# A graph layer on one core: the rows of a chosen block are selected in three pieces over three steps, and the program's end gets a new order

## The reference

```
edge_index = stack([src, dst]);  x_j = x[src];  x_i = x[dst]
msg = concatenate([x_i, x_j - x_i], axis=-1)
h = relu(msg @ W1 + b1)          # 64 -> 64
h = relu(h @ W2 + b2)            # 64 -> 128
h = relu(h @ W3 + b3)            # 128 -> 64
m = h @ W4 + b4                  # 64 -> 32
s   = segment_sum(m, dst, N)
cnt = segment_sum(ones, dst, N)
x = layernorm(x + s / maximum(cnt, 1))
```

## Time and profile before

| | us |
|---|---|
| median of 3 executions | 2438.02 (2434.82 to 2444.65) |
| the profiled execution | 2446.31 |
| its span, first to last instruction | 2444.5 |
| mean granted TensorE clock | 0.79 of full |
| TensorE matmuls busy | 1712.6 (70%) |
| GpSimd busy | 1128.2 (46%) |
| VectorE busy | 952.4 (39%) |
| ScalarE busy | 621.9 (25%) |

### The profile page before, as it was taken

One profiled execution on the slowest core, in us unless ns is written; L12 is line 12 of the kernel. 1 busy time (PEld: TensorE's weight loads), 2 busy tenths in 40 slices (PEclk: granted clock), 3 DMA queues, 4 the chain that ended last, 5 costly groups with the idle time before them and its releaser, 6 DMA issues.

```text
span 2444.5 us, 39204 instructions
## 1 busy us (share of the span) xinstructions
PE 1712.6 (70%) x13107; PEld 1103.7 (45%) x13107; DVE 952.4 (39%) x3083; ACT 621.9 (25%) x945; POOL 1128.2 (46%) x1168
## 2 busy tenths in 40 slices
PE   2242777777786777777677867777777777777796
PEld 2111544554454545454444554454544454544463
DVE  3673333333333333343333333333333333333354
ACT  2233222222222222222222222222222222222243
POOL 5276354445545453545455444545454544454412
PEclk7565887888878877888788888788888878788897
DMA  5343533443433434343434443443443343434341
GB/s 127 98 116 91 174 99 109 132 138 98 122 114 102 139 105 126 98 142 100 139 98 122 117 141 99 119 117 97 145 124 113 95 142 100 137 99 127 115 126 29
DMA packets 189929, 283.06 MB, mean 116 GB/s; under 512 B 84614, under 2 KB 90169, under 8 KB 189156
## 3 DMA queue, kind: packets, MB, share of 16 engines
q1 hardware_dynamic: 152341, 241.67, 31.9%
q0 software_dynamic: 36704, 37.00, 7.7%
q10 hardware_dynamic: 682, 1.85, 0.3%
HBM read 266.51 MB, written 13.73 MB: 115 GB/s over the span
## 4 chain that ended last, share of the span: by engine, by line
PE 40%; another core or an unknown queue 29%; issue 15%; DVE 8%; ACT 4%; DVEq 2%; DMA 1%; SPq 1%; POOL 0%; ACTq 0%; POOLq 0%
PE ps L954 21%; PE ps L978 4%; PE ps L986 4%; PE ps L994 2%; PE ps L1009 2%; DVE region L1384 2%; ACT work L713 2%; PE ps L898 2%; PE ps L968 2%; DVEq L1397 1%; PE ps L1006 1%; PE ps L916 1%; ACT work L721 1%; DVE region L1351 1%
## 5 line engine op out<-in xcount | busy, mean ns | idle before, releaser
L584 POOL DMA_INDIRECT xj<-z_rows,src_t x1107 | 1072.6, 969 | 1186.2 <-PE ps L916 682.0
L954 PE MATMUL ps<-region,x_p 128*96 128x150 bf16 (+53 forms) x5876 | 537.2, 256 | 244.9 <-issue 234.0
L954 PEld LDWEIGHTS ps<-region,x_p 128*96 128x96 bf16 x5876 | 479.2, 159 | 345.1 <-issue 337.3
L1351 DVE TENSOR_SCALAR region<-region,cst 128x1565 bf16<-128x1565 int16 (+6 forms) x416 | 242.3, 636 | 285.0 <-PE ps L954 151.2
L1366 DVE COPY work<-ps 128x512 f32<-128x512 f32 x194 | 133.4, 688 | 541.3 <-remote 380.7
L986 PE MATMUL ps<-work,w3s 128*64 128x512 f32 x784 | 327.0, 748 | 17.8 <-ACT work L721 14.5
L721 ACT ACTIVATE work<-ps,b2s 128x512 f32<-128x512 f32 x392 | 260.5, 686 | 249.4 <-remote 217.1
L994 PE MATMUL ps<-cst,work 128*128 128x128 f32 x784 | 150.5, 323 | 243.8 <-ACT work L728 224.1
L728 ACT ACTIVATE work<-ps,b3s 128x512 f32<-128x512 f32 x196 | 134.7, 687 | 720.1 <-remote 647.0
L978 PE MATMUL ps<-work,w2s 64*128 64x512 f32 x784 | 243.5, 700 | 39.2 <-ACT work L713 38.3
L713 ACT ACTIVATE work<-ps,b1s 128x512 f32<-128x512 f32 x196 | 134.7, 687 | 385.1 <-PE ps L898 312.2
(11 more groups left out here) (153 smaller groups left out, 907.6 us busy)
## 6 DMA issues: line engine op xcount, KB each, us to landing
dstb<-dst_rows SPq DMA_DIRECT2D x196, 252.0 KB
region<-src_rows SPq DMA_DIRECT2D x104, 391.2 KB
region<-src_rows SPq DMA_DIRECT2D x52, 407.2 KB
region<-src_rows SPq DMA_DIRECT2D x52, 403.2 KB
region<-src_rows SPq DMA_DIRECT2D x52, 376.2 KB
region<-src_rows SPq DMA_DIRECT2D x52, 375.8 KB
region<-src_rows SPq DMA_DIRECT2D x52, 374.0 KB
region<-src_rows SPq DMA_DIRECT2D x52, 366.2 KB
```

The source lines that it names most:

```text
L584: pool.indirect_dma_start(out=xj[:, u, j % UT, j // UT, 0:w], out_offset=None, in_=rows, in_offset=bass.IndirectOffsetOnAxis(ap=cols[:, j: ...
L954: chosen = nc.tensor.matmul(ps[0:XP, XBANK[h], lo - h * UE:hi - h * UE], xb[:, a, :], hot[:, q % QN, at + lo:at + hi], start=not begun[h], ...
L1351: nc.vector.tensor_scalar(hot[:, q % QN, 0:CW[c]], spread[:, q % QE, 0:CW[c]], cst[:, C_PID:C_PID + 1], None, ALU.is_equal).then_inc(s_hot, 1)
```

## The change

The selection of a chosen block's rows is cut into three pieces of chunks, `PIECES = [(0, 1, 2), (3, 4, 5), (6, 7)]`. TensorE does piece 0 in the step two before the block's own, piece 1 in the step before, both behind `sum_window` and ahead of layer 3, and piece 2 where the whole selection stood. VectorE builds the one-hots of a piece at the end of the step before, and SyncE loads the windows of the following block piece by piece, ahead of its other loads.

At the program's end: the engines meet only if another pass follows; each chunk's four matmuls of `messages` read four runs of neighbouring nodes, and `turn_messages` writes them back to their places; the short chunk comes last instead of first; every second chunk's addition of x goes from GpSimd to VectorE; and TensorE does matmuls whose result nobody reads (`stay_busy`) in the last steps and before the messages. A new assertion holds the chosen blocks at least three steps apart.

```diff
+PIECES = [(0, 1, 2), (3, 4, 5), (6, 7)]
-CHUNKS = [(0, NC % CH)] + [(NC % CH + CH * n, CH) for n in range(NC // CH)]
+CHUNKS = [(CH * n, CH) for n in range(NC // CH)] + [(NC - NC % CH, NC % CH)]
...
 (SyncE)
             def step(s):
-                if is_sorted(s) and STEPS[s] + 1 < SB:
-                    for c in range(CN - QN):
-                        load_windows(STEPS[s] + 1, QN + c)
+                for lead in range(3):
+                    if s + lead < S_N and is_sorted(s + lead) and STEPS[s + lead] + 1 < SB:
+                        for c in PIECES[2 - lead]:
+                            load_windows(STEPS[s + lead] + 1, c)
...
-                if s + 1 < S_N and is_sorted(s + 1) and STEPS[s + 1] + 1 < SB:
-                    for c in range(QN):
-                        load_windows(STEPS[s + 1] + 1, c)
...
-                sp.wait_ge(s_acc, added_by(S_N - 1))
-                sp.wait_ge(s_arrive, 4)
-                sp.sem_clear(per_pass)
-                sp.sem_inc(s_open, WIN)
                 with sp.If(off + WIN < end):
+                    sp.wait_ge(s_acc, added_by(S_N - 1))
+                    sp.wait_ge(s_arrive, 4)
+                    sp.sem_clear(per_pass)
+                    sp.sem_inc(s_open, WIN)
...
+            sp.wait_ge(s_acc, added_by(S_N - 1))
             sp.dma_start(cnt, sums[H3:H3 + 1, 0:N].rearrange("a (p c) -> a p c", c=NC)).then_inc(s_count, 16)
...
 (GpSimd)
             for n in range(len(CHUNKS)):
-                add_x(n)
+                if n % 2 == 0:
+                    add_x(n)
...
 (TensorE)
-            def selected_x(s):
+            def selected_x(s, piece):
...
-                free_x(s)
-                if b == 0:
+                if piece == 0:
+                    if copies_by(s - 1):
+                        pe.wait_ge(s_xc[0], copies_by(s - 1))
+                    if b:
+                        pe.wait_ge(s_xc[1], b)
+                    begun[0] = begun[1] = False
...
-                for c in range(CN):
+                for c in PIECES[piece]:
...
+            def stay_busy(n):
+                for k in range(n):
+                    nc.tensor.matmul(ps[0:XP, 0, :], xb[:, 0, :], x_p[:, 0:512], start=True, stop=True)
             def step(s):
                 if s < S_N:
                     if is_sorted(s):
-                        selected_x(s)
+                        selected_x(s, 2)
...
+                stay_busy({S_N + 1: 3}.get(s, 0))
                 if 2 <= s <= S_N + 1:
                     turn_layer3(s - 2)
+                stay_busy({S_N: 4, S_N + 1: 2, S_N + 2: 8}.get(s, 0))
                 if s >= 3:
                     sum_window(s - 3)
+                for lead in (1, 2):
+                    if s >= AHEAD and s + lead < S_N and is_sorted(s + lead):
+                        selected_x(s + lead, 2 - lead)
...
+            stay_busy(7)
+            pe.wait_ge(s_acc, added_by(S_N - 1))
             messages(0)
...
 (VectorE)
-                if s < S_N and is_sorted(s):
-                    for c in range(QN, CN):
-                        build_hot(STEPS[s], c)
...
-                for lead, some in ((2, (0, 1)), (1, (2, 3, 4))):
-                    if s + lead < S_N and is_sorted(s + lead):
-                        for c in some:
+                for lead in (1, 2, 3):
+                    if s >= AHEAD and s + lead < S_N and is_sorted(s + lead):
+                        for c in PIECES[3 - lead]:
                             build_hot(STEPS[s + lead], c)
...
+                    if n % 2:
+                        dve.wait_ge(s_m, n + 1)
+                        nc.vector.tensor_tensor(zc[:, cs, :], zc[:, cs, :], xc[:, cs, :], ALU.add).then_inc(s_z[1], 1)
```

More of the change, by code:

```diff
@@ L54 @@
     STEPS.append(k if n in SORTED_AT else SB + n - k)
+assert all(b - a >= 3 for a, b in zip(SORTED_AT, SORTED_AT[1:])) and FIRST_SORTED >= AHEAD + 3
 assert sorted(STEPS) == list(range(S_N)) and STEPS[-1] == S_N - 1
@@ L278, in build @@
         s_fin, s_m, s_z, s_sq, s_var, s_std, s_rstd, s_y, s_out = (
-            sem("messages"), sem("mean_message"), sem("z_ready"), sem("z_squared"), sem("var_ready"), sem("std_ready"),
+            sem("messages"), sem("mean_message"), [sem("z_ready_gpsimd"), sem("z_ready_vector")], sem("z_squared"), sem("var_ready"), sem("std_ready"),
             sem("rstd_ready"), sem("y_ready"), sem("out_stored"))
@@ L599, in _ @@
                 pool.dma_reset(range(s_gath[0].num, s_gath[-1].num + 1))
-                end_of_pass(pool, off)
-                pool.sem_inc(s_begun, 1)
                 with pool.If(off + WIN < end):
+                    end_of_pass(pool, off)
+                    pool.sem_inc(s_begun, 1)
                     for g in range(early):
@@ L609, in add_x @@
                 pool.wait_ge(s_m, n + 1)
-                nc.gpsimd.tensor_tensor(zc[:, at, :], zc[:, at, :], xc[:, at, :], ALU.add).then_inc(s_z, 1)
+                nc.gpsimd.tensor_tensor(zc[:, at, :], zc[:, at, :], xc[:, at, :], ALU.add).then_inc(s_z[0], 1)
             def normalise(n):
@@ L777, in _ @@
                     step(s)
-                end_of_pass(act, off)
-                act.sem_inc(s_begun, 1)
                 with act.If(off + WIN < end):
+                    end_of_pass(act, off)
+                    act.sem_inc(s_begun, 1)
                     for s in range(AHEAD):
@@ L806, in _ @@
                     copy_wide(n + 2)
-                act.wait_ge(s_z, n + 1)
+                act.wait_ge(s_z[n % 2], n // 2 + 1)
                 nc.scalar.activation(zq[:, at, :], zc[:, at, :], ACT.Square).then_inc(s_sq, 1)
@@ L935, in gathered_x @@
                 add_dst(s)
-            def selected_x(s):
+            begun = [False, False]
+            def selected_x(s, piece):
                 b = STEPS[s]
-                free_x(s)
-                if b == 0:
+                if piece == 0:
[4 more added lines that the diff above has]
+                    begun[0] = begun[1] = False
+                if b == 0 and piece == 0:
                     pe.wait_ge(s_xb, 16)
                     pe.wait_ge(s_maskc, 1)
-                begun = [False, False]
                 last0 = max(a for a in range(NB) if WINDOWS[a][0] < UE)
-                for c in range(CN):
+                for c in PIECES[piece]:
                     q = b * CN + c
@@ L1046, in _ @@
                     step(s)
-                end_of_pass(pe, off)
                 with pe.If(off + WIN < end):
+                    end_of_pass(pe, off)
+                    pe.sem_inc(s_begun, 1)
                     for s in range(AHEAD):
                         step(s)
-            by_node = sums[:, 0:N].rearrange("f (p c) -> f c p", c=NC)
+            by_node = sums[:, 0:N].rearrange("f (p c) -> f p c", c=NC)
             def messages(n):
@@ L1059, in messages @@
                 for i in range(4):
-                    nc.tensor.matmul(ps[i * O:(i + 1) * O, n % 2, 0:w // 4 * NP], w4s[:, :], by_node[:, c0 + i:c0 + w:4, :],
+                    at = c0 + i * (w // 4)
+                    nc.tensor.matmul(ps[i * O:(i + 1) * O, n % 2, 0:w // 4 * NP], w4s[:, :], by_node[:, :, at:at + w // 4],
                                      start=True, stop=True).then_inc(s_strip[i], 1)
@@ L1066, in turn_messages @@
                     pe.wait_ge(s_m, n - 5)
-                for j in range(CHUNKS[n][1] // 4):
-                    turned = nc.tensor.transpose(ps[0:NP, 2 + n % 6, j * 4 * O:(j + 1) * 4 * O], wide[:, n % 2, j, :], ident)
+                w = CHUNKS[n][1]
+                prod = ps[0:NP, 2 + n % 6, 0:w * O].rearrange("p (i j f) -> p j i f", i=4, f=O)
+                for j in range(w // 4):
+                    turned = nc.tensor.transpose(prod[:, j, :, :], wide[:, n % 2, j, :], ident)
                 turned.then_inc(s_fin, 1)
+            stay_busy(7)
+            pe.wait_ge(s_acc, added_by(S_N - 1))
             messages(0)
@@ L1457, in _ @@
                 dve.wait_ge(s_acc, added_by(S_N - 1))
-                end_of_pass(dve, off)
-                dve.sem_inc(s_begun, 1)
                 with dve.If(off + WIN < end):
+                    end_of_pass(dve, off)
+                    dve.sem_inc(s_begun, 1)
                     moves = [0]
```

2 lines of the change are left out of this document (1 added, 1 removed).

## The result

| | before | change |
|---|---|---|
| median, us (19 executions each) | 2430.15 | 2410.76 |
| lowest | 2405.83 | 2390.89 |
| highest | 2446.78 | 2636.36 |
| profiled execution | 2446.31 | 2442.93 |
| its span | 2444.5 | 2441.1 |

The ratio is 0.9906, 95% interval 0.9883 to 0.9928: the change is faster by 0.9%, and the forecast was 4.3%.

What follows compares the result with a forecast made beforehand. The bound was taken as the gathers' time plus what TensorE cannot start under them. From the profiled 2446.3 us, -97 (pieces, -1.9 us per block, 50 blocks) and -9 (program's end) gave 2340 us, range 2280 to 2440.

Steps and rivals of the forecast that it cites:

- Windows without a piece, 11.8 us: Gathered steps with no piece and no chosen block would stay at 11.8 us.
- The block's window, -2.6 us: Window with a chosen block: piece 1 and layer 3 hidden, layer 2 left over; -2.6 us, bounds -4.6 and -1.5.
- The window with piece 0, +0.7 us: Gathered window given piece 0: 67 records fit, only the next transposes left over, +0.66 us, taken as +0.7.
- the band of 64 to 70: Records TensorE starts in a block's window before the hold ends: sum 16, layers 8, selection 40 to 46.
- my own bound: Upper bound for the window with piece 0: both layers and the transposes left over, 2.9 us.
- Cost of the clock: Splitting the selection in the gathered loop was taken to leave TensorE's clock as it is.
- my signs of being wrong: Piece 0 windows over 13.5 us, clock after the hold under 0.7, or total moving while block windows don't.
- The fourth rival: After the hold in block windows, pieces leave TensorE at its lower clock: +1.2 us per block, 2497 us; chance 0.07.
- The end, -9 us: Program's end: last addition to span's end 28.8 to 22 us, -6.8; better clock before messages, -2.2.
- the second rival: Pieces only shift TensorE's left-over work between windows; the end alone gains, 2437 us; chance 0.13.
- the third: Layers and transposes left over in piece 0 windows, both layers in block windows: +2.1 us, 2542 us; chance 0.11.
- The fifth rival: Source loads, not gathers, cause TensorE's gaps; spread, block windows fall to 15.8 us, total 2052 us; chance 0.03.

Runs made afterwards that it cites:

- e5: The kernel before, unchanged, run again on a slower chip: 2439.16 us, one execution.
- e12: The change with pieces 0 and 1 behind layer 2 instead of ahead of layer 3, slower chip: 2398.07 us, ratio 0.9783 to before.
- e6: The change, unchanged, on a slower chip: 2496.44 us, ratio 1.0185 to the kernel before.
- e17: The change with pieces of 29, 45 and 39 matmuls, all behind layer 2, second slower chip: 2377.81 us, ratio 0.9723 to before.
- e9: The kernel before with only the new program's end, selection in one piece, slower chip: 2436.87 us, ratio 0.9957.
- e1: The kernel before with only the new program's end, selection in one piece, faster chip: 1562.53 us, ratio 0.9968.
- e7: The kernel before with all gathers of the loop left out, slower chip: 1491.81 us, one execution.
- e8: The kernel before with four of a step's eight gathers left out, slower chip: 1732.22 us, one execution.

## Why the prediction was off

**Windows without a piece, 11.8 us: right** (11.5 to 11.7), on the chips of the result and of e5 to e12.

**The block's window, -2.6 us: right in the mean, in part by luck.** -2.2 us in the result, -1.7 in e6. The step counts sum 16, piece 1 45 and layer 3 4 under the gathers and layer 2 left over; in the result layer 3 was left over too in 34 of 50 windows (22.4 us), and got in in 16 (19.2 us). Against the 23.6 us of before these are -1.2 and -4.4 us, near the two bounds (-1.5 and -4.6); the forecast 21 us is the mean of two kinds, and few windows have it.

**The window with piece 0, +0.7 us: this is the step that failed.** It read "Window with piece 0: sum 16, piece 39, layers 8, next transposes 4: 67 records. That is in the band, at its edge. I take the next transposes as left over". Measured: +2.4 us in the result, +2.7 in e6. When the issue of the last gather began, layer 2 had not started in 49 of 50 windows, and layer 3 had not in 10 (16.0 us; 13.6 where it had). So 67 records do not fit, and the band of 64 to 70 was read too high. I had added both layers and a sum to the selections of two blocks, 40 and 46. The sum stands ahead of the window, before the first gather at 1202.55:

```profile
1201.02 1.93 PE L1009 MATMUL ps<-region,work 128*65 128x42 f32 x16
1202.87 2.08 PE L986 MATMUL ps<-work,w3s 128*64 128x512 f32 x4
```

Counted alike in all 50 windows with a block of before, from the beginning of the sum to the end of the last issue, TensorE starts 61 records in the mean (16, 8 and 37 of the selection; 33 to 130), of them 42 behind the first gather. In the change's windows with piece 0 it starts 57: the sum, piece 0 and part of layer 3. It is so whether the window follows a block's (23 of them, 58 records) or a plain one (27, 55), in which the sum and some 13 matmuls of the piece have started before the first gather. e6 has 57 too. Left over were then part of layer 3, layer 2 and the transposes, near my own bound (both layers and the transposes, 2.9 us), and layer 2 at the price of the low clock (1.92 us instead of 1.13).

**Cost of the clock: taken as none, and it had one.** The clock in the loop fell from 0.80 to 0.77, and from issue's end to the release it is 0.66 in the windows with piece 0 (0.71 before; in e6 0.65, in e5 0.76). Two of my signs of being wrong were met in these windows: over 13.5 us, and a clock under 0.7 behind the hold. The fourth rival had this (layer 3 +0.9 us) for the block's window; it belonged to the window before. The Trainium skill, "TensorE: Matmul & The Clock Gate", section "Loop structure matters more than you think", has it that matmuls with long waits between them run at the slow clock, and the rows agree: 1.92 us for layer 2 where it had been 1.13. But the clock alone doesn't decide: e12 and e17 have three pieces too, their clock in the same place is lower still (0.51), and they gain 2.2 and 2.8%. With the pieces behind the layers, what is left over there is selection matmuls and transposes.

**The end, -9 us: right.** e9 has it alone: 0.9957, which is 10.6 us (4.7 to 16); on the faster chip e1 gives 5.0 us. From the last addition to the end it is 23.3 us (22 forecast): an addition on VectorE costs 1.28 us while GpSimd does one too, and 0.69 us alone (the two rows L1530), and I had taken 0.69. How much of the result is the end's, no run on the result's chip separates.

**Together.** The forecast was -97 - 9. In the result it came to -19, of which the end explains about 10 by e9, and the pieces would be the other 9, so the second rival (nothing from the pieces) was nearest. On the slower chip of e6 it was the third (both layers left over and the hold's end waited for, decided where windows with piece 0 pass 14.4 us): they have 14.42 there, and the change is 1.85% slower. Layer 3 had not started in 26 of 50 when the last issue began, instead of 10; in most windows it starts within a microsecond or so of that moment, and at the end of the issue it is 8 and 5. The term that I put at +0.7 stood at the point where the sign turns; one microsecond in these 50 windows is 50 us, and the whole result is 19.

**The fifth rival** (gathers don't hold TensorE) is false on the slower chips: without the gathers, and with all source loads, TensorE is free (e7). On the faster ones its first half is true, and its time still isn't reached, since GpSimd's ten microseconds a step are the bound there. The rule of the Trainium skill, "SBUF — State Buffer", section "SBUF: two separate sides", that transfers and compute cannot slow each other, holds in e7 with its source loads and in e1 with the gathers too (0.02 us from end to count). With gathers on the chip of the result it is 2.43 us; whether that speaks against the rule isn't shown, since no run separates the transfers of a gather from GpSimd's issue of it.

What stays open: why some chips hold TensorE under indirect DMAs and two don't, whether that is lasting, and whether it is GpSimd's issue or the transfers that does it. That wasn't tried.

## What to carry to other kernels

When an engine's completions come late, put work that nobody waits for yet behind the work that is waited for: on one slower chip the same pieces cost 1.9% ahead of the layers (e6) and gained 2.2% behind them (e12). A capacity read from two windows is no capacity: count it in all of them, from the same record to the same event, before a plan is laid at its edge. And run a kernel whose bound is such a hold on a second chip before a schedule is tuned to it: here the kernel before took 1567 or 2447 us on different chips, and the same change was 0.9% faster, 1.9% slower or worth nothing.

## What the runs showed of the hardware

- The kernel before takes 1566 to 1567 us on two chips and 2430 to 2449 us on the others, though single instructions are alike: a gather's issue takes 0.95 us, layer 2 at the full clock 1.13 us, 113 selection matmuls in one run 6.47 us, in before and in e1.
- On the slower chips TensorE's semaphore counts come 1.5 to 2.6 us behind the modelled end of its work in the mean while eight gathers a step run (2.4 in before and e5), and 0.8 us with four (e8); those of ScalarE and VectorE 0.01 us. Without gathers TensorE's come after 0.02 us there too (e7).
- The hold lasts past the last issue: in plain steps the next first gather is issued 1.6 to 2.1 us behind the last one's end with eight gathers a step and 1.5 us with four.
- An addition of 125 x 512 on VectorE takes 0.69 us alone, and longer when it starts while one of GpSimd's (1.27 us) is under way: 0.80 us with 0.25 us of it still to go, 1.00 with 0.46 (e6), 1.28 with 0.73.
